# Parking the residual in quarter transfers instead of eight whole rows, in a hybrid transformer kernel on eight cores

## The reference

```python
x = x + attn_a(layernorm(x))      # 16 heads of queries, one shared head of keys and values
x = x + ffn(layernorm(x))         # two layers: windowed attention, then a gated MLP
x = x + attn_b(layernorm(x))      # low-rank causal attention over 16 heads
x = x + ffn(layernorm(x))         # the same weights again
```

## Time and profile before

| | us |
|---|---|
| median of 2 runs | 10965.89 (10951.84 to 10979.94) |
| the profiled execution | 10925.52 |
| its span, first to last instruction, slowest core (core 4) | 10924.0 |
| spans of the eight cores | 10810.0 to 10924.0 |
| busy on core 4: TensorE matmuls | 6026.5 |
| VectorE | 3228.1 |
| ScalarE | 2755.4 |
| GpSimd | 549.2 |

### The profile page before, as it was taken

One profiled execution on the slowest core, in us unless ns is written; L12 is line 12 of the kernel. 1 busy time (PEld: TensorE's weight loads), 2 busy tenths in 40 slices (PEclk: granted clock), 3 DMA queues, 4 the chain that ended last, 5 costly groups with the idle time before them and its releaser, 6 DMA issues.

```text
span 10924.0 us, 88373 instructions; the slowest of 8 cores (10810.0 to 10924.0 us)
## 1 busy us (share of the span) xinstructions
PE 6026.5 (55%) x20128; PEld 1884.9 (17%) x20128; DVE 3228.1 (30%) x6033; ACT 2755.4 (25%) x3584; POOL 549.2 (5%) x648
## 2 busy tenths in 40 slices
PE   1167763557664566653444444443556675557775
PEld 0021211112221122210111111111112221112221
DVE  0130015442214432124333333334433122442222
ACT  0037661231101321002333333332132010231110
POOL 2100002100001100000000000000200000100000
PEclk9978886679886778875666666566667876677775
DMA  9800001014340014440000000001003442003443
GB/s 113 85 9 1 1 31 20 1 27 107 97 117 5 1 40 101 110 108 6 5 5 5 5 5 6 6 6 51 1 1 76 108 102 67 1 1 75 103 101 108
DMA packets 1038946, 496.23 MB, mean 45 GB/s; under 512 B 885056, under 2 KB 931392, under 8 KB 1035360
## 3 DMA queue, kind: packets, MB, share of 16 engines
q1 hardware_dynamic: 883264, 412.95, 15.5%
q0 software_dynamic: 134464, 52.44, 5.1%
q10 hardware_dynamic: 20736, 25.19, 0.7%
HBM read 504.84 MB, written 67.12 MB: 52 GB/s over the span
## 4 chain that ended last, share of the span: by engine, by line
PE 33%; DMA 19%; DVE 17%; ACT 15%; issue 10%; POOL 3%; DVEq 1%; another core or an unknown queue 1%; SPq 1%; ACTq 1%; POOLq 0%
DMA PT<-w2C 8%; DMA KD<-w1C 6%; PE SP L1243 5%; ACT PT L618 4%; DMA BC<-x 3%; PE PVa L1185 3%; PE PVb L1195 2%; ACT PT L1624 2%; PE PVa L1022 1%; ACT PT L1003 1%; PE SP L1185 1%; PE SP L1195 1%; PE SP L1054 1%; DVE PT L1012 1%; PE SP L804 1%
## 5 line engine op out<-in xcount | busy, mean ns | idle before, releaser
L1243 PE MATMUL SP<-B,PT 128*128 128x512 bf16 (+1 forms) x2816 | 965.1, 483 | 534.8 <-DMA PT<-w2C 516.1
L804 PE MATMUL SP<-WSLOT,B 128*128 128x512 bf16 x1536 | 461.2, 468 | 453.3 <-DVE B L792 262.1
L618 ACT ACTIVATE PT<-SP 128x1024 bf16<-128x1024 f32 x512 | 524.4, 1024 | 295.9 <-PE SP L604 183.1
L1003 ACT ACTIVATE PT<-SP 128x1024 bf16<-128x1024 f32 x448 | 458.9, 1024 | 374.2 <-PE PVb L1029 200.1
L1243 PEld LDWEIGHTS SP<-B,PT 128*128 128x128 bf16 (+1 forms) x2816 | 266.9, 110 | 1242.8 <-issue 1162.8
L1256 DVE SCALAR_TENSOR_TENSOR X<-SP,B2C,X 128x512 f32<-128x512 f32 x128 | 96.2, 751 | 1199.5 <-PE SP L1243 1189.2
L1012 DVE TENSOR_TENSOR PT<-PT,MASKS 128x1024 bf16<-128x1024 bf16 x448 | 319.9, 714 | 349.6 <-ACT PT L1003 339.7
L1624 ACT ACTIVATE PT<-SP 128x1024 bf16<-128x1024 f32 x320 | 327.8, 1024 | 303.4 <-PE SP L1606 225.2
L497 DVE TENSOR_TENSOR AR<-PVa,TMP 64x512 bf16<-64x512 f32 x96 | 65.5, 683 | 1086.3 <-ACT TMP L493 1086.3
L980 PE MATMUL SP<-B,AR 64*128 64x512 bf16 x448 | 222.0, 521 | 258.9 <-ACT PT L1003 172.8
L818 ACT CAST AR<-SP 128x512 bf16<-128x512 f32 x64 | 37.5, 586 | 1286.4 <-PE SP L804 1005.7
(11 more groups left out here) (261 smaller groups left out, 10760.8 us busy)
## 6 DMA issues: line engine op xcount, KB each, us to landing
KD<-w1C SPq DMA_DIRECT2D x672, 256.0 KB, 3.8
PT<-w2C SPq DMA_DIRECT2D x672, 256.0 KB, 2.6
w1C<-fw POOLq DMA_DIRECT2D x84, 256.0 KB, 25.2
xpark<-X ACTq DMA_DIRECT2D x16, 1025.0 KB, 12.6
WSLOT<-wqkvC SPq DMA_DIRECT2D x4, 3072.0 KB, 11.5
BC<-xpark SPq DMA_DIRECT2D x44, 256.0 KB, 3.3
w2C<-fw POOLq DMA_DIRECT2D x42, 256.0 KB, 57.9
BC<-x SPq DMA_DIRECT2D x128, 64.0 KB, 7.7
```

The source lines that it names most:

```text
L618: se = sop(lambda e, sl=sl: e.activation(PT[:, 2 * sl:2 * sl + 2, :], SP[:, 1024 * sl:1024 * sl + 1024], AF.Exp), waits=wE)
L804: sh=sh, ring=ring: e.matmul(PB[bank][:, :], ZBr(c, ring, 1 + 128 * q + sh, 128), WSLOT[:, c, 512 * part:512 * (part + 1)], start=(c == 0) ...
L1003: se = sop(lambda e, sl=sl: e.activation(PT[:, 2 * sl:2 * sl + 2, :], SP[:, 1024 * sl:1024 * sl + 1024], AF.Exp, scale=8.0), waits=wE)
L1243: ot=ot, oi=oi: e.matmul(PB[oi][:, :], bass.AP(PT, 1024 * par + 128 * ot, [[4 * 512, wid], [1, 128]]), B[0:wid, 512 * pr:512 * (pr + 1)], ...
```

## The change

Instead of eight stores of whole chunks, block after block is stored: for each of the 4 blocks eight DMAs of 128 x 512 float32 (256 KB each, rows of 2048 bytes), 32 in all, again on ScalarE's queue. The two guard columns of X are no longer stored; nothing reads them back. Each block has a semaphore of its own, `d0` to `d3`, and `mat(tb)` waits for its own block's only. Only the very first DMA carries the wait for VectorE. GpSimd waits for the four semaphores one after another. Both feed-forward phases run this code.

```diff
     def phase_ffn(app):
         barrier()
         pt_guard = [0]
-        d_park = 0
-        for c in range(NCH):
-            d_park = dma("scalar", S["sp"], xpark[c, :, :], X[:, c, :],
-                         waits=[(S["v"], S["v"].n)])
-        p.do("gpsimd", None, waits=[(S["sp"], d_park)])
+        psem = [S["d0"], S["d1"], S["d2"], S["d3"]]
+        d_park = [0] * NTB
+        for tb in range(NTB):
+            lo = 1 + 512 * tb
+            for c in range(NCH):
+                d_park[tb] = dma("scalar", psem[tb],
+                                 xpark[c, :, lo:lo + 512],
+                                 Xs(c, lo, 512),
+                                 waits=[(S["v"], S["v"].n)] if (tb == 0 and
+                                                               c == 0) else [])
+        for q in range(NTB):
+            p.do("gpsimd", None, waits=[(psem[q], d_park[q])])
         v_mat = entry_ln(lambda c, lo: Xs(c, lo, 512),
-                         extra_mat_waits=lambda tb: [(S["sp"], d_park)])
+                         extra_mat_waits=lambda tb: [(psem[tb], d_park[tb])])
         v_z0 = v_mat[NTB - 1]
```

## The result

| | us |
|---|---|
| before, median of 37 runs | 10925.94 |
| after, median of 38 runs | 10991.12 |
| ratio, after to before | 1.0048, 95% interval 1.0025 to 1.007 |
| the profiled execution after: span of its slowest core, core 1 | 11009.6 |

The change makes the kernel slower by 0.5%, some 52 us (27 to 77). That is within the 2% named in the prediction and yet clear of zero, because there are many runs.

A forecast was written before the change was run, and what follows sets the result against it. The prediction took one core's serial phases as the bound, with chains of short waiting steps at the two feed-forward entries. Longer issuing there, +11.6 and +9.8, together +21.3 us on 10965.89, gave 10987 us, range 10956 to 11032.

The forecast's parts named there:

- The wait that the change removes: Block 0's first normalising subtraction waiting for all of X to be stored: 0 us on core 4, at most 2.54 us anywhere.
- The issues gate the squares, one for one: In both feed-forward entries, ScalarE's first square starts only after the last store issue, 0.15 us behind it.
- The price of an issue: ScalarE's time per new store issue at each entry: 0.60 us, thus 32 issues take 19.2 us per entry.
- the floor of 0.43: Lower bound per store issue on ScalarE, from issues into an idle queue: 0.43 us, so 32 take at least 13.8 us.
- the drain of 0.73 to 0.84: Old 8 MB store's time to last landing, 26.9 and 23.5 us, per quarter-size transfer: 0.84 and 0.73 us an issue.
- The floor pace: Rival: entry stores issue at 0.43 us each, 13.8 us per entry; +10.5 us in all, 10976; chance 0.22.
- The full pace: Rival: 1.30 us per entry store whatever its size, 41.6 us per entry; +66.1 us in all, 11032; chance 0.11.
- Stalls: Rival: every entry store issue stalls, 4.53 us each, 145 us per entry; +273 us in all, 11239; chance 0.02.
- The early release pays: Rival: block 0's normalisation no longer waits for the other blocks' stores; alone 10963; chance 0.03, without visible issue cost.
- The rule: Skill page on DMA issue: initiating is usually small relative to the DMA, so the entries' sum would be near 0 us.
- the prediction's 83 us: Page's fit, 2.0 us fixed plus bytes at 436 GB/s, paid one after another: 32 x 2.6 us per entry.

The follow-up runs named there:

- repeated run: The changed kernel, unaltered, profiled and timed once more beside another version on one chip, 5 rounds; ratio to the kernel before 1.0052 (1.0008 to 1.0095).

## Why the prediction was right, and where not

**The wait that the change removes is worth nothing on the path.** Right. It was 0 us on core 4 before; with the new issues in front it is hardly reached any more, as the run with one wait for all blocks shows (1.64 us in one entry of 16). What I missed is its size in other executions: I put 2.54 us as the most, from eight cores of one execution; the runs with whole transfers show up to 6.7 and 8.9 us. Even that would not have turned the sign.

**The issues gate the squares, one for one.** Right, and shown from both sides: on SP's queue and in the idle stretches the square comes at 4.7 to 5.8 us and the whole cost is gone. The first square came at +33.0 and +20.9 us (core 1), 0.15 us behind the last issue, where I had +19.4.

**The price of an issue: the term that was mis-sized.** I took 0.60 us, between the floor of 0.43 and the drain of 0.73 to 0.84. On core 1 it is 20.75 / 32 = 0.65 in the second entry and 32.84 / 32 = 1.03 in the first. Core 1, the first 24 and the last seven issues of the first entry, then the last 27 of the second:

```profile
L214 ACTq DMA_DIRECT2D xpark<-X x24: 346/572/1514, 1589.3 to 1604.6; - x24
...
L214 ACTq DMA_DIRECT2D xpark<-X x7: 1126/2070/2940, 1606.7 to 1619.3; - x7
...
L214 ACTq DMA_DIRECT2D xpark<-X x27: 488/630/663, 7581.5 to 7598.5; - x27
```

In the second entry the pace stays at 0.63 us to the end of the row; in the first it is the last issues that are held, for 1.1 to 2.9 us each. Over the cores there are six entries of the first kind, 0.64 to 0.77 us an issue, and ten of the other, 0.76 to 1.04. Nine of 16 entries took over 27 us to issue, the most that I had written for them.

The error is in my upper bound for the drain: I took the time in which the old transfers drain, 26.9 and 23.5 us, for the time in which the new ones would. From first issue to last landing core 1 now needs 1619.3 + 17.4 - 1589.3 = 47.4 us in the first entry and 7598.5 + 10.4 - 7578.4 = 30.5 us in the second. My sum was +11.6 and +9.8 = +21.3 us; the means over the cores are +22.1 and +14.4 = +36.5, more than the +33.3 of the drain's own upper end. The repeated run gives +30.7 by the same measure.

**What was not in it: the neighbour.** The spread of the issue times over the cores goes with when the next core parks. Taking the same pairs, and the starts of their issues from the start of each core's span: in the changed kernel, where the two starts lie 4.6 to 13 us apart (five pairs) the issues take 24.4 to 33.2 us, and where they lie 20 to 31 us apart (three pairs) 20.6 to 24.6. In the first entries all four pairs lie within 13 us, in the second only one does, and the first entry lost more. With 64 transfers it is the same: 52.9 to 64.6 us in the six close pairs, 41.9 to 47.6 in the two others. With one wait for all blocks all eight pairs lie within 14 us, and the issues take 24.6 to 34.8 us, in the second entries as in the first. In the repeated run the second entries lie 26 to 38 us apart and take 20.8 to 22.1 us, and the longest row of all, 37.6 us, is in a pair 1.3 us apart.

Two more signs say the same. In the 64 entries of the four runs with these 32 transfers (changed, repeated, SP's queue, one wait) the time to the last landing falls as the starts of a pair move apart, with a correlation of -0.94; with the cores paired in any of six other ways it is -0.34 to -0.44. And with the eight whole transfers the block 0 wait is there in all 22 entries whose pair starts within 12.1 us, and in two of the 26 others, by 0.78 and 0.35 us. Two cores together seem to drain hardly faster than one alone: in the run with 4096-byte rows cores 6 and 7 start their second entry 0.3 us apart and need 49.0 us for 16.8 MB, 342 GB/s, while 8.4 MB in 23.5 us on core 4 before are 357 GB/s. All this is a pattern over pairs, not an experiment, and it supposes that the cores' spans start together; a run that holds one core of a pair back was not made. What the neighbour slows is open too.

**The rivals.** The floor pace (10976) fell: even rows of eight take 0.56 us an issue. The full pace, 1.30 us, was reached by none of the entries, but the worst (37.55 us in the repeated run, 1.17 each) come near it. It rested on the first issues of the old row, which is not steady: its median is 1.07 us. Stalls of microseconds did come, up to 3.8 us for one issue in a first entry (core 0), but not on every issue. The early release pays: not here.

**The rule.** That the time to initiate a DMA is usually small beside the DMA (the Trainium skill, "DMA: Bandwidth & Descriptors", "Issuing engines are not separate DMA queues") does not hold for the row as a whole: on core 1 the issues fill 20.75 of the 30.5 us to the last landing. For one transfer it does, 0.65 us against a landing after 8.2 us (median of that entry). The advice of the same page to coalesce ("Rules for kernel authors") points the right way here only ahead of the squares, and for the reason that these runs give: not the bandwidth, but the engine that issues. Even there the 1 MB and 2 MB transfers by block stayed slower than before, and the 256 KB ones cost nothing where nobody stood behind them. The fit behind the prediction's 83 us ("Anatomy of one DMA") is given by the page for DMAs issued from GpSimd; 32 issues on ScalarE took 20.6 to 33.2 us.

**The total.** The forecast of 10987 us lies near 10991.12, and partly by luck: it was set on the median of two runs, 10965.89, where 37 runs give 10925.94; the step of +21 us was too small against the +52 us (27 to 77) of the ratio, and the base was 40 us too high. The two errors cancel. On the base of 37 runs the same step would have given 10947, below the range as well as below the result.

## What to carry to other kernels

A DMA costs its issuing engine's queue time, and that is free only if nothing that others wait for stands behind it: before cutting a transfer, look at what is next in that queue. Finer waits help only if the finer transfers are issued where they hold nobody up; here the same 32 issues cost 12 to 25 us an entry ahead of the squares and nothing in ScalarE's idle stretches or on SP. The length of a row of issues is not a fixed price times their number: where the data fell behind, the last issues of the row were held for 1.1 to 2.9 us each.

## What the runs showed of the hardware

- The time to issue a row of park transfers of 8 MB, in us, all on ScalarE: 8 of 128 rows of 8200 bytes, 7.1 to 10.0; 16 of 128 x 4096, 12.4 to 18.4; 32 of 128 x 2048, 20.6 to 33.2 (20.5 to 37.6 in the repeated run); 64 of 128 x 1024, 41.9 to 64.6; 8 of 512 x 2048, 13.8 to 25.9; 4 of 1024 x 2048, 10.3 to 16.2; 32 of 32 x 8200, 27.2 to 32.2. Neither the number of issues nor that of rows gives all of them.
- A single issue can hold its engine for 10.0 us, with 1024 rows behind three others of that kind; the first of the four takes 0.37 to 0.41 us.
- With rows of 4096 and 8200 bytes an issue takes about 1.0 to 1.3 us, and less, not more, while the neighbouring core is storing (eight whole transfers in 7.0 to 7.9 us against 8.2 to 10.0).
- Two cores that store 8 MB each at about the same time seem to slow each other, where their numbers are neighbours: 37.6 us with the starts 1.3 us apart against 20.6 with them 31 us apart, for the same 32 issues; a pattern only, as said above.
